# GpSimd forms two of the row blocks of products in the recurrence of a delta-rule layer

## The reference

```python
def step(carry, x):                       # lax.scan over the 32 tokens
    S_f, S_s = carry                      # (batch 32, heads 16, 64, 64) each
    S_f = fdt * S_f;  S_s = sdt * S_s
    err_f = vt - kt @ S_f;  err_s = vt - kt @ S_s
    S_f = S_f + bt * outer(kt, err_f);  S_s = S_s + bt * outer(kt, err_s)
    S_fc = cap(S_f + rf * S_s)            # S / max(1, ||S|| / 64)
    S_sc = cap(S_s + rf * S_f)
    ot = fgt * (qt @ S_fc) + sgt * (qt @ S_sc)
    return (S_fc, S_sc), ot
```

## Time and profile before

| | us |
|---|---|
| median of 3 runs (lowest, highest) | 1902.64 (1901.27, 1902.86) |
| profiled execution, its own time | 1900.15 |
| its span | 1898.4 |
| VectorE busy, whole span | 1199.3 |
| GpSimd busy, whole span | 94.8 |
| VectorE on r_prod (L1058), 158 instructions | 83.6 |

### The profile page before, as it was taken

The page is one execution under the profiler, slowest core; times in us unless marked ns, Lnnn a source line. Parts: engine busy times, 40 slices in busy tenths (PEclk is TensorE's granted clock), DMA queues, the critical chain, the costliest instruction groups (busy, mean ns, idle before and its releaser), DMA issues. The chain is left out here.

```text
span 1898.4 us, 22234 instructions
## 1 busy us (share of the span) xinstructions
PE 1548.0 (82%) x7255; PEld 1150.0 (61%) x7255; DVE 1199.3 (63%) x2643; ACT 711.4 (37%) x1361; POOL 94.8 (5%) x261
## 2 busy tenths in 40 slices
PE   6999999999899999049200089479999999999998
PEld 3888888888677776013000088456666666666664
DVE  4366555666233797999999755435665555555555
ACT  2333333333354545001000222135555555555552
POOL 0000000000000000012112100040000000000003
PEclk9999999999899999569655579579999999999999
DMA  3211011110213541450100231075515505325004
GB/s 117 78 34 33 17 33 33 33 33 0 93 63 32 93 87 35 65 178 1 44 0 0 67 83 34 1 282 205 178 39 205 205 22 195 133 95 188 29 17 139
DMA packets 116152, 152.93 MB, mean 81 GB/s; under 512 B 47072, under 2 KB 67936, under 8 KB 116064
## 3 DMA queue, kind: packets, MB, share of 16 engines
q1 hardware_dynamic: 110336, 137.68, 24.2%
q0 software_dynamic: 2560, 8.39, 1.3%
q10 hardware_dynamic: 3168, 5.77, 0.8%
HBM read 250.25 MB, written 31.33 MB: 148 GB/s over the span
## 5 line engine op out<-in xcount | busy, mean ns | idle before, releaser
L1679 DVE TENSOR_TENSOR gl<-w_gu,gh 128x2048 fp32r<-128x2048 f32 x138 | 290.6, 2106 | 16.5 <-ACT gh L1614 16.4
L1614 ACT CAST gh<-w_gu 128x2048 fp32r<-128x2048 f32 x138 | 242.2, 1755 | 58.9 <-DMA w_gu<-in_up_proj 49.0
L1569 PE MATMUL bank<-w_d,hT 128*128 128x512 f32 x506 | 242.4, 597 | 10.1 <-ACT hT L1638 10.1
L1546 PE MATMUL bank<-gh,xh 128*128 128x512 f32 (+1 forms) x552 | 219.1, 397 | 10.5 <-DVE xl L1670 8.8
L1712 DVE TENSOR_TENSOR hid<-silu,bank 128x256 f32<-128x256 f32 x138 | 55.0, 398 | 259.1 <-ACT silu L1627 259.1
L1548 PE MATMUL bank<-gh,xl 128*128 128x512 f32 (+1 forms) x552 | 207.2, 375 | 0.0
L1547 PE MATMUL bank<-gl,xh 128*128 128x512 f32 (+1 forms) x552 | 206.9, 375 | 0.0
L1175 PE MATMUL bank<-o_v,xnT 128*128 128x64 f32 x256 | 36.1, 310 | 177.9 <-DMA o_v<-scratch_v_rows 177.9
L1175 PEld LDWEIGHTS bank<-o_v,xnT 128*128 128x128 f32 x256 | 35.8, 227 | 178.7 <-DMA o_v<-scratch_v_rows 178.7
L1569 PEld LDWEIGHTS bank<-w_d,hT 128*128 128x128 f32 x506 | 91.6, 189 | 83.7 <-issue 55.3
L1627 ACT ACTIVATE silu<-bank 128x256 f32<-128x256 f32 x138 | 50.6, 367 | 212.8 <-PE bank L1548 212.8
(11 more groups left out here) (293 smaller groups left out, 3057.9 us busy)
## 6 DMA issues: line engine op xcount, KB each, us to landing
w_gu<-in_gate_proj SPq DMA_DIRECT2D x46, 1024.0 KB
w_gu<-in_up_proj SPq DMA_DIRECT2D x46, 1024.0 KB
w_d<-in_down_proj SPq DMA_DIRECT2D x46, 1024.0 KB
w_gu<-in_gate_proj SPq DMA_DIRECT2D x23, 768.0 KB
w_gu<-in_up_proj SPq DMA_DIRECT2D x23, 768.0 KB
w_d<-in_down_proj SPq DMA_DIRECT2D x23, 768.0 KB
ctx_raw<-in_ctxT SPq DMA_DIRECT2D x32, 385.5 KB, 3.7
scratch_gram<-gram SPq DMA_DIRECT2D x8, 768.0 KB, 3.4
```

What stands on the lines that cost most here:

```text
L1546: pe.matmul(bank, xh[s % 2][:, k, :], hi, start=(k == 0), stop=False)
L1569: mm = pe.matmul(bank, hT[n % 2][:, c, :], w_d[:, b * (BLK // P) + c, :], start=(b == 0 and c == 0), stop=(b == NB - 1 and c == cs[-1]))
L1614: nc.scalar.copy(gh[n % RING][:, :, :, 0:bw].rearrange("p k a f -> p (k a) f"), w_gu[:, :, :, b * BLK:b * BLK + bw].rearrange("p k a f -> ...
L1679: nc.vector.tensor_tensor(gl[n % RING][:, :, :, 0:bw].rearrange("p k a f -> p (k a) f"), w_gu[:, :, :, b * BLK:b * BLK + bw].rearrange("p ...
```

## The change

In each step with three blocks GpSimd forms the products of blocks 0 and 1, in each with four those of blocks 1 and 2 (`shared`). VectorE forms the rest and all sums, and the sums of GpSimd's blocks come last (`order`). Two semaphores are new: `pr_done`, counted up by `weights`, on which GpSimd and VectorE wait, and `pool_made`, on which VectorE's sums of those blocks wait. In GpSimd's list the products for nxt stand ahead of the wait for the cap of step t.

```diff
+        def shared(nxt):
+
+            return {3: (0, 1), 4: (1, 2)}.get(len(range(0, nxt + 1, W)), ()) if nxt < N else ()
+
+        def product(eng, nxt, x, a):
+            rows, parts = blocks_of(nxt)
+            lo, hi, cols = rows[x]
+            return eng.tensor_tensor(parts[x][:, a], G[:, :, lo:hi, 2, 0:cols],
+                                     bc(pr[nxt % 2][:, a, :, None, 0:cols], [SG, hi - lo, cols]), ALU.mult)
...
             def _(pool):
...
                 for t in range(N):
                     u, m, n = t % PSI, t + 1, t * POOL_STEPS
+                    if shared(t + 1):
+                        pool.wait_ge(pr_done, t + 1)
+                        for x in shared(t + 1):
+                            for a in range(2):
+                                product(nc.gpsimd, t + 1, x, a).then_inc(pool_made, 1)
...
                     if nxt < N:
-                        need(pr_ready)
...
+                        dve.wait_ge(pr_done, nxt)
+                        rows, parts = blocks_of(nxt)
+                    first = [x for x in range(len(rows)) if x not in shared(nxt)]
+                    order = first + list(shared(nxt))
+                    halves = [(x, a) for x in first for a in range(2)]
+                    made = {}
+
+                    def products(n):
+
+                        for x, a in halves[:n]:
+                            made[x] = mark(product(nc.vector, nxt, x, a))
+                        del halves[:n]
+
+                    def sums(n):
+
+                        if n < len(order):
+                            x = order[n]
                             lo, hi, cols = rows[x]
...
+                            if x in made:
+                                need(made[x])
+                            else:
+                                dve.wait_ge(pool_made, from_pool + 2 * (shared(nxt).index(x) + 1))
...
                     need(terms)
                     norms = mark(red(n2[:, :, :].rearrange("p r s -> p s r"), zz[:, :, :, :], AX.X, ALU.add))
-                    made[1] = products(1, 1)
+                    products(1)
                     need(norms)
                     ts(nm[:, :, :], n2[:, 0:3:2, :], 0.0, None, ALU.max).then_inc(nm_ready, 1)
-                    products(2, 0)
-                    made[2] = products(2, 1)
-                    products(3, 0)
-                    made[3] = products(3, 1)
+                    products(len(halves))
```

More of the change, by code:

```diff
@@ L940, in recurrence @@
         nm_ready, root_ready, blank_out = sem("r_nmr"), sem("r_rootr"), sem("r_blank_out")
+        pr_done, pool_made = sem("r_prd"), sem("r_pool_made")
         g_in, g_done, g_used, blocks_zero = sem("g_in"), sem("g_done"), sem("g_used"), sem("blocks_zero")
@@ L946, in bc, with blocks_of @@
             return ap.to_broadcast([P] + shape)
+        def blocks_of(nxt):
+            rows, parts, at = [], [], 0
+            for x in range(0, nxt + 1, W):
+                lo, hi, cols = x, min(x + W, nxt + 1), min(x + W, nxt)
+                size = 2 * SG * (hi - lo) * cols
+                rows.append((lo, hi, cols))
+                parts.append(prod[:, at:at + size].rearrange("p (a s i j) -> p a s i j", a=2, s=SG, i=hi - lo))
+                at += size
+            return rows, parts
+        def shared(nxt):
[5 more added lines that the diff above has]
+                                     bc(pr[nxt % 2][:, a, :, None, 0:cols], [SG, hi - lo, cols]), ALU.mult)
         with nc.Block() as block:
@@ L1037, in weights @@
                 def weights(t):
-                    return mark(tt(pr[t % 2][:, :, :, 0:t], psi[(t - 1) % PSI][:, :, :, 0:t], bc(G[:, None, :, 0:t, 0, t], [2, SG, t]), ALU.mult))
+                    tt(pr[t % 2][:, :, :, 0:t], psi[(t - 1) % PSI][:, :, :, 0:t], bc(G[:, None, :, 0:t, 0, t], [2, SG, t]), ALU.mult).then_inc(pr_done, 1)
                 need(spread_states(0))
-                pr_ready = weights(1)
+                weights(1)
+                from_pool = 0
                 z_ready = dots_ready = None
@@ L1045, in _ @@
                     u, m, nxt = t % PSI, t + 1, t + 1
-                    rows, parts, at = [], [], 0
+                    rows, parts = [], []
                     if nxt < N:
-                        need(pr_ready)
[L1049 to L1056, removed]
-                            lo, hi, cols = rows[x]
[L1058 to L1064, removed]
+                        dve.wait_ge(pr_done, nxt)
[11 more added lines that the diff above has]
+                            x = order[n]
+                            lo, hi, cols = rows[x]
+                            if x in made:
+                                need(made[x])
+                            else:
+                                dve.wait_ge(pool_made, from_pool + 2 * (shared(nxt).index(x) + 1))
                             return mark(red(vp[:, :, :, lo:hi].rearrange("p a s i -> p (a s) i"),
@@ L1067, in sums @@
                         return summed
-                    made = [None] * 4
                     if dots_ready is not None:
@@ L1072, in _ @@
                         raw = mark(red(zr[:, :, :], dots[:, :, :, :, 0:t].rearrange("p a b s t -> p (a b) s t"), AX.X, ALU.add))
-                        products(0, 0)
+                        products(1)
                         need(raw)
@@ L1076, in _ @@
                     else:
-                        products(0, 0)
-                    made[0] = products(0, 1)
+                        products(1)
+                    products(1)
                     if z_ready is not None:
@@ L1082, in _ @@
                                     bc(z[:, :, :].rearrange("p k s -> p s k")[:, :, None, :], [SG, 3, NZ]), ALU.mult))
-                    products(1, 0)
+                    products(1)
                     need(terms)
                     norms = mark(red(n2[:, :, :].rearrange("p r s -> p s r"), zz[:, :, :, :], AX.X, ALU.add))
-                    made[1] = products(1, 1)
+                    products(1)
                     need(norms)
                     ts(nm[:, :, :], n2[:, 0:3:2, :], 0.0, None, ALU.max).then_inc(nm_ready, 1)
-                    products(2, 0)
-                    made[2] = products(2, 1)
-                    products(3, 0)
-                    made[3] = products(3, 1)
+                    products(len(halves))
                     summed = None
@@ L1120, in _ @@
                         need(psi_done)
-                        pr_ready = weights(nxt + 1)
+                        weights(nxt + 1)
+                    from_pool += 2 * len(shared(nxt))
 def outputs(nc, d, ps, ident, x_nat, gate, wo, wo_in, outw, spare):
```

## The result

The changed kernel takes 1923.65 us, the median of 4 runs (1923.37 to 1924.22), beside 1901.95 us for the kernel before (4 runs, 1899.15 to 1902.86). The ratio is 1.0117 with a 95% interval of 1.0099 to 1.0135: slower, by 21.7 us. The prediction said 1919.5 us, 17.0 us slower.

A forecast was written before the change was run, and what follows sets the result against it. VectorE's own instruction list was taken to bound the kernel. Four-block steps +15.2, three-block steps +2.8 and moves -1.0 summed to +17.0 us on the 1902.64 us median: 1919.6, given as 1919.5, range 1898 to 1936.

The forecast's parts named there:

- What bounds it: Recurrence: each step lasts as long as VectorE's instruction list, so a microsecond on VectorE is a microsecond of the kernel.
- What is removed: Products leaving VectorE: 1.86 us a three-block step, 2.94 a four-block step, 38.4 us in all.
- unfilled dependences: Three-block steps: norms and r_nm follow with nothing between, costing about 0.11 us each for the result ahead of them.
- Moves: Larger sum behind the cap covers more of GpSimd's output chain in the first few three-block steps: -1.0 us, +0 to -2.
- GpSimd's duration: GpSimd's products take 2.08 ns a column on 0.19 us: 0.72, 1.25 and 1.79 us for 256, 512 and 768 columns.
- the ends 1.66 and 2.6: GpSimd's bounds in ns a column: +4.4 us (1907) at 1.66, +32.6 us (1935) at 2.6.
- rivals 3 and 4: GpSimd fast, 1.4 to 1.66 ns a column: -3 to +5 us, chance 0.13; slow, 2.6 and above: +33 us, 0.12.
- Turns: Two-input VectorE instructions and GpSimd instructions reading SBUF exclude each other for whole instructions; 4.7 us standing a four-block step.
- Four blocks: Steps of nxt 24 to 31: 2.9 us removed, 4.7 of standing added, +1.9 us a step, +15.2 us in all.
- Three blocks: Steps of nxt 16 to 23: +0.35 us a step, +2.8 us in all.
- r_nm ... 4.3: Three-block step of nxt 21: r_nm done 4.3 us after the weights, against 4.0 before, GpSimd's fourth product beside the sums.
- Rivals 1 and 2: Engines do not exclude each other: -30 us, chance 0.06; VectorE goes first, GpSimd entering only during reductions: -9 us, 0.09.

The follow-up runs named there:

- e2: Changed kernel with GpSimd's products left out and no wait for them, VectorE's list and order kept: 1869.48 us (one run).
- e6: Against the kernel before: GpSimd forms only block 0 (three-block steps) or block 1 (four-block), started on r_nm, beside VectorE's sums: 1894.77 us, ratio 0.9969.
- e8: Changed kernel with GpSimd's clearing of xnT moved ahead of its products: 1923.93 us (one run).
- e4: Changed kernel with r_nm written by a reduction instead of the one-input max in the eight three-block steps: 1918.31 us, 1.0094 of before.
- e1: Kernel before, VectorE's list whole, with GpSimd forming the same two blocks of products again into an unread spare tensor: 1975.41 us (one run).
- e3: Changed kernel with GpSimd writing zeros where it formed products, reading nothing from SBUF, VectorE still waiting for them: 1875.08 us (one run).
- e7: e6 with GpSimd's 3.5 us clearing of xnT in step 29 moved ahead of its products: 1891.92 us, ratio 0.9948 of before.

## Why the prediction was right, point by point

- **What bounds it.** Right: the difference of the spans (24.1 us) is that of VectorE's list (23.06) and a microsecond in front of it. By parts the +17.0 us missed 4.3 us up to the first sum of the three-block steps, 0.8 there in the four-block steps, 0.9 in the moves and the 1.0 in front: with them it is the 24.1 of the spans. All four misses point the same way, so the total owes nothing to errors that cancel. It owes 1.2 us to luck: the prediction writes 1.9 and 0.35 us a step where its own figures, 8.2 - 6.4 and 4.3 - 4.0, give 1.8 and 0.3.
- **What is removed.** 38.4 us predicted less 8 x 0.22 for the unfilled dependences, 36.6; e2 shows 13.3 + 24.8 = 38.1 us less. Of these 36.5 lie up to the first sums, as worked out, and 1.6 behind them.
- **Moves: -1.0 predicted, -0.1 measured.** Behind the first sums the three-block steps gain 0.4 us. The four-block steps gain where nothing was forecast, 0.25 to 0.3 us each at nxt 26 to 28 (r_sc costs 0.08 us of VectorE's time instead of 0.33 to 0.39), and lose 1.15 at nxt 30 to the clearing of xnT.
- **GpSimd's duration.** 2.08 ns a column on 0.19 us gave 0.72, 1.25 and 1.79. Unhindered, two of 256 take 1.40 us together and two of 512 2.50 (e6); a held one of 768 needs 1.65 us from its release, 1.60 of it streaming at 2.08 ns. The plain add was the right row to go by; the ends 1.66 and 2.6 (rivals 3 and 4) fall.
- **Turns.** Right in kind and nearly in place. The four-block step was worked out as 8.2 us to the point where the sums begin and took 8.4. One turn was different: GpSimd's fourth product went ahead of the first product of block 3, not behind it (2.47 us for that product), in all eight steps. So the reduction for the norms, which was to run beside the fourth, came behind it (1053.94 to 1054.13), and these 0.2 us are the difference.
- **Four blocks: +15.2 predicted, +16.4 measured, +16.0 of it up to the first sum.** Measured are 2.0 us a step there (8.37 - 6.38 at nxt 29). The whole steps cost 1.7 to 2.1 us each but for nxt 30. That one cost 3.1, of which 1.15 lies behind the start of its first sum, where r_nm stands for the clearing of xnT (e8 takes these 1.15 back and gives up 0.3, because the products start later). The prediction had passed over it with "the cap comes later than they end"; it had asked only who waits for the cap.
- **Three blocks: +2.8 predicted, +7.1 measured up to the first sum (+6.7 with what follows).** This is the term that was mis-sized. Up to the terms the step worked out for nxt 21 is right: zz ends 3.89 us behind the weights (946.75), 3.85 predicted. The step "r_nm ... 4.3", with "GpSimd's fourth runs beside the sums", took r_nm for free of GpSimd because it has one input. It stands for the fourth product, which ends at 5.04 (5.0 predicted), and ends at 5.06 itself. With 0.82 us instead of 0.16 that is 0.66 us a step, 5.3 us in eight. e4 takes this away and leaves +1.8 up to the first sum, below the predicted +2.8; the whole stretch gains 4.74, since 0.5 is lost again at the max of the root. The Trainium skill (SBUF — State Buffer, "Who interferes with whom") lists this form too: `tensor_scalar` may use the shared ports for a single input. Here r_nm at 0.82 us and r_root at 3.90 us agree. The prediction had used the rule on two inputs alone.
- **Rivals 1 and 2** fall with e1 and with the timeline: in none of the eight four-block steps do two VectorE multiplies pass a waiting product, except the pair z and product (0,1) that the prediction named.

What stays open is why a write-only GpSimd instruction and one that reads hold a one-input VectorE instruction differently. In e3, and in the changed kernel behind r_nm held by the clearing (1071.00), the reduction behind the held instruction starts 0.08 us after it and only ends no earlier; in the changed kernel, behind r_nm held by a product (947.10), it starts when r_nm ends (947.83). Nor is it shown why the clearing went ahead of a standing r_root in e6. It wasn't tried either whether the reciprocal of the cap is held; in all these kernels it met no GpSimd work.

## What to carry to other kernels

An engine that looks idle is only free if its work can run beside the bound engine's: before moving elementwise work from VectorE to GpSimd, look at a place where the two already meet and compare durations with and without the meeting. Two-input multiplies and the one-input max instructions stood for GpSimd's whole instruction here, reductions did not. The products paid when they were placed under VectorE's sums (e7, 0.9948 of before) and lost when placed under its multiplies (1.0117). The two kernels differ in number too, since e7 gives GpSimd two products a step and not four; four under the sums, or two under the multiplies, were not run. Busy shares and lists of waits do not show such standing; durations of the same form do.

## What the runs showed of the hardware

- A two-input VectorE instruction held by a reading GpSimd one ends behind it by little more than the time that its columns take: 0.03 us for 16 columns (z 1049.42 behind 1049.39), 0.23 for 120 (zz 1051.63 behind 1051.40), 0.73 for 696 (1054.01 behind 1053.28). The one-input max of 8 columns ends 0.03 behind (r_root 1029.04 behind 1029.01).
- A held GpSimd product of 768 columns ends 1.65 us behind the VectorE instruction that held it (1051.40 behind 1049.75), 1.60 of it by 2.08 ns a column.
- A GpSimd write of constants holds no two-input VectorE instruction (zz 0.36 us beside it), but holds the end of a one-input one, up to 3.90 us for 8 columns (r_root, e6).
- A VectorE reduction is not held by GpSimd's products: 8 columns take 0.16 us (e4), one of 512 and one of 1536 columns 2.34 us together (e6). It only can't end ahead of a held instruction in front of it (1.46 us for 512 columns behind r_nm at 1071.00).
